# A sparse-attention layer on one core: query rows made by a product in the first steps, and another order around tile 0 in the last ones

## The chip, the cores and the metric

The kernel runs on 1 core of one Trainium2 chip. The metric is the device time in microseconds of one execution. The engines are TensorE (PE, with its weight loads on PEld), VectorE (DVE), ScalarE (ACT), GpSimd (POOL) and the engine that issues DMAs (SP). POOL also issues DMAs; its queue is called q0 here, SP's q1.

## What is computed

One layer of a graph transformer on 4096 nodes with 256 features, 8 heads of 32, fp32. The adjacency matrix is sparse: an edge (i, j) exists with a chance that falls with i and j, so the first rows have many neighbours and the last few.

```
mask = adj + eye(n)
q, k, v = h @ Wq.T + bq, h @ Wk.T + bk, h @ Wv.T + bv        # 8 heads of 32
scores = einsum(q, k) / sqrt(32), -1e9 where mask == 0
ctx = softmax(scores) @ v
h1 = layer_norm(h + ctx @ Wo.T + bo) * g1 + b1
h2 = layer_norm(h1 + relu(h1 @ W1.T + b1) @ W2.T + b2) * g2 + b2
```

## The kernel before

The 4096 rows are 32 tiles of 128. Up to about 66 us the key and value rows of all tiles are projected and stored in a table in HBM (`kv_table`), and the query rows of the first tiles in `q_table`. Then 19 **steps** follow (`STEPS`, numbered 0 to 18). Steps 0 to 3 treat tiles 4 to 7, one each; steps 4 to 15 two tiles each; steps 16, 17 and 18 the tiles 1, 2 and 3, with 3, 3 and 2 units. A unit is a stretch of columns of one tile. Tile 0, the densest, has 14 units and is no step of its own: it is worked off beside the others.

For each step:
- POOL loads 128 rows of the adjacency matrix as bytes (`load_adj`, a DMA that casts, two to three steps ahead), and VectorE **searches** them (`find_dve`, lines 533 and 537) for up to eight neighbours a row and unit. `columns_dve` and `spill_dve` make lists of them. The first neighbour of a row is treated as *aligned* with the row; the rest spill over and are packed as *edges*.
- TensorE and ScalarE make a selection matrix `rt` for packed slots (`starts_pe` L882, `distance_act`, `rt_dve`), then `lists_pe` (L889) and `cols_dve` give the column numbers of the edges, `rows_act` their row numbers, and `onehot_act` the transposed selection.
- POOL **gathers** with indirect DMAs: `gather_aligned` (L1084), `gather_edges` (L1096: key and value rows of the edges) and `gather_queries` (L1104: the query row of each edge, from `q_table`), one instruction a unit. SP loads the tile's own rows and queries (`load_own`).
- VectorE multiplies queries by keys and sums (`edge_scores_dve`, L687; `own_scores_dve`, L702), TensorE brings the edge scores to their rows (`ell_pe`, L901), VectorE takes the maximum and subtracts (`masked_dve`), ScalarE the exponential, VectorE the reciprocal (`norm_probs_dve`). TensorE hands maximum and reciprocal back to the edges (`tr_pe`, L909); VectorE weights the value rows (`own_sum_dve` with L783, `edge_weight_dve` with L792), and TensorE adds them up (`sum_pe`, L927 and L930).

Each engine runs its instructions in the written order; a wait stops all behind it. In steps 0 to 2 TensorE also has the query projections of the later tiles (`project_q`, four pairs of tiles a step, L1869 and L1872). From step 4 on it has the dense part of finished groups of four tiles, a **job**: attention output (L1153, with the residual through L1141), a transpose (L1163), the first feed-forward product (`post_pe_ff`, eight parts, L1173) and the second (`post_pe_out`, one a tile, L1186). They are cut into the gaps between a step's sparse matmuls (`dense(gap)`); two steps make one job. ScalarE takes the results (L1223), VectorE the statistics (L1243), POOL the root and the gain and bias of the second norm (`post_pool_gain` L1291, `post_pool_final` L1295).

**Tile 0** is scored in seven pieces of two units, in steps 8 to 14 (`score0_dve`, `masked0_dve`; their gathers in steps 6 to 12). In step 15 VectorE takes the maximum over its 1800 scores a row (`below0_dve`, L838), subtracts it (L840), ScalarE takes the exponential, and VectorE the sum (`norm0_dve`, L846). At the end of step 15 TensorE hands it to the 14 units (`tr0_pe`, L959), in step 16 and 17 VectorE weights the rows (`weight0_dve`, L868 and L871), and in step 17 TensorE adds them up (`sum0_pe`, L971, two halves back to back). In steps 16 to 18 the jobs 5 and 6 are finished by tables of their own (`late_ff`, `late_out`); S in the code is 16, W is 6. After step 18 two small jobs of two tiles follow, and `last_dve` ends the last.

## Time and profile before

| | us |
|---|---|
| three runs | 538.21, 535.16, 538.68 |
| median | 538.21 |
| the profiled execution: its time | 536.31 |
| its span, first to last instruction | 534.1 |
| PE busy | 474.5 (89%) |
| DVE busy | 389.7 (73%) |
| POOL busy | 270.3 (51%) |
| ACT busy | 216.0 (40%) |

The span lies 2.2 us under its execution's time. "Busy" is the sum of instruction times on an engine; a matmul at half clock counts longer. The granted TensorE clock over the span is 0.936 of full speed; the lows lie in steps 0 to 4 and 16 to 18. A row by stretch (rows 2) gives the stretch, its length, then the busy us of PE, PEld, DVE, ACT and POOL with the number of instructions each, the granted TensorE clock, the DMA share and GB/s. A row of a timeline gives start, duration, engine, line and operands. The waits in brackets name what ended the idle time of an engine just before an instruction.

### The profile page before, as it was taken

The numbers are of one execution on the slowest core, as the hardware profiler recorded it, in microseconds if no ns is written. First come the engines' busy times: TensorE is split into PE (matmuls) and PEld (weight loads), VectorE is DVE, ScalarE is ACT, GpSimd is POOL, SyncE is SP. The second block draws the span as 40 slices with busy tenths as digits, with TensorE's granted clock in tenths as the row PEclk, the third lists the DMA queues.
The fourth block names the chain that finished last, engine by engine and source line by source line (L and its number), as shares of the span: only waits on it lengthen the run. The fifth ranks groups of instructions, "written<-read, shape, count | busy, mean of one in ns | idle before, by whom it ended". The sixth has DMA issues, their size and how long they took to land.

```text
span 534.1 us, 7363 instructions
## 1 busy us (share of the span) xinstructions
PE 474.5 (89%) x2274; PEld 373.1 (70%) x2274; DVE 389.7 (73%) x1067; ACT 216.0 (40%) x533; POOL 270.3 (51%) x374
## 2 busy tenths in 40 slices
PE   5999978894389989999999999999999986999893
PEld 4888867783376677589578668758847864778682
DVE  0648825979788869799989979979969798713103
ACT  1243431443535334723624543373373436223530
POOL 7544454544334346777576657665455557300402
PEclk9999997986577989999999999999999888999997
DMA  7999869999979978999989898994673435100101
GB/s 181 282 285 311 233 205 221 288 255 233 281 157 214 173 168 140 236 223 198 228 144 221 201 171 205 138 242 149 114 160 97 129 91 152 56 1 1 40 0 43
DMA packets 42571, 91.66 MB, mean 172 GB/s; under 512 B 4888, under 2 KB 20632, under 8 KB 42400
## 3 DMA queue, kind: packets, MB, share of 16 engines
q0 software_dynamic: 16512, 55.60, 53.3%
q1 hardware_dynamic: 24224, 33.69, 18.1%
q10 hardware_dynamic: 1792, 1.85, 1.0%
q8 instruction: 20, 0.33, 0.3%
q14 instruction: 23, 0.19, 0.1%
HBM read 123.09 MB, written 16.80 MB: 262 GB/s over the span
## 4 chain that ended last, share of the span: by engine, by line
PE 62%; DVE 14%; issue 9%; ACT 6%; POOL 5%; DMA 4%; POOLq 0%; ACTq 0%; DVEq 0%
PE ps L1173 17%; PE ps L1186 14%; PE ps L1853 10%; PE ps L1153 6%; PE ps L927 2%; PE ps L1141 2%; DVE adj_bytes L533 2%; DVE adj_bytes L537 2%; DMA work<-q_table,row_of 2%; PE ps L971 2%; PE ps L930 1%; PE ps L1163 1%; POOL slots L1096 1%; DMA early<-in_wqkvT 1%; ACT early L1233 1%
## 5 line engine op out<-in xcount | busy, mean ns | idle before, releaser
L1186 PE MATMUL ps<-w,xT_all 128*128 128x256 f32 x512 | 118.4, 385 | 4.3 <-ACT xT_all L1223 2.6
L1173 PE MATMUL ps<-xT_all,w 128*128 128x512 f32 (+1 forms) x288 | 117.9, 554 | 2.6 <-ACT xT_all L1223 1.4
L1186 PEld LDWEIGHTS ps<-w,xT_all 128*128 128x128 f32 x512 | 95.8, 192 | 17.9 <-ACT xT_all L1223 3.8
L1096 POOL DMA_INDIRECT slots<-kv_table,col_of x54 | 53.4, 989 | 68.6 <-DVE col_of L613 53.9
L1173 PEld LDWEIGHTS ps<-xT_all,w 128*128 128x128 f32 x288 | 52.3, 192 | 47.2 <-issue 40.1
L1084 POOL DMA_INDIRECT slots<-kv_table,found x48 | 51.0, 1063 | 50.1 <-PE ps L930 26.1
L1223 ACT ACTIVATE xT_all<-ps,col_table 128x512 f32<-128x512 f32 (+1 forms) x72 | 45.8, 642 | 57.1 <-PE ps L1173 56.0
L1853 PE MATMUL ps<-early,xT_all 128*128 128x256 f32 x256 | 59.7, 394 | 6.1 <-DMA early<-in_wqkvT 6.1
L1853 PEld LDWEIGHTS ps<-early,xT_all 128*128 128x128 f32 x256 | 49.9, 198 | 14.0 <-DMA xT_all<-in_xT 4.7
L533 DVE MAX8 adj_bytes<-adj_bytes 128x8 f32<-128x1024 f32 (+5 forms) x40 | 38.2, 973 | 17.4 <-DMA adj_bytes<-in_adj 17.4
L1104 POOL DMA_INDIRECT work<-q_table,row_of x40 | 42.1, 1052 | 13.8 <-issue 13.8
L1243 DVE BATCH_NORM_STATS2 stats<-ps 128x6 f32<-128x256 f32 x62 | 22.2, 418 | 29.9 <-PE ps L1141 29.8
L1153 PE MATMUL ps<-wo,xT_all 128*128 128x256 f32 x128 | 39.3, 435 | 4.1 <-issue 4.1
L1282 POOL TENSOR_TENSOR rstd<-mv,eps_col 128x4 f32<-128x4 f32 (+1 forms) x17 | 5.8, 343 | 71.8 <-DVE mv L1249 71.5
L1039 ACT ACTIVATE xT_all<-ps,col_table 128x256 f32<-128x256 f32 (+1 forms) x38 | 14.4, 432 | 65.9 <-PE ps L930 65.9
L537 DVE FIND_INDEX8 adj_bytes<-adj_bytes 128x8 uint32<-128x1024 f32 (+5 forms) x40 | 38.9, 979 | 0.0
L927 PE MATMUL ps<-work,slots 128*128 128x128 f32 x160 | 29.0, 293 | 9.7 <-DVE slots L792 8.0
L1869 PE MATMUL ps<-early,xT_all 128*128 128x256 f32 x128 | 37.4, 419 | 0.0
L1608 POOL TENSOR_TENSOR slots<-slots,early 128x512 f32<-128x512 f32 x16 | 20.3, 1266 | 28.3 <-ACT slots L1700 28.3
L927 PEld LDWEIGHTS ps<-work,slots 128*128 128x128 f32 x160 | 24.6, 205 | 11.3 <-DVE slots L792 8.8
L1700 ACT COPY slots<-ps 128x1024 f32<-128x1024 f32 x16 | 16.2, 1012 | 39.3 <-PE ps L1853 39.3
L1153 PEld LDWEIGHTS ps<-wo,xT_all 128*128 128x128 f32 x128 | 25.1, 217 | 7.1 <-issue 4.6
(185 smaller groups left out, 856.4 us busy)
## 6 DMA issues: line engine op xcount, KB each, us to landing
adj_bytes<-in_adj POOLq DMA_DIRECT2D x31, 512.0 KB
kv_table<-slots POOLq DMA_DIRECT2D x7, 1024.0 KB, 13.0
xT_all<-in_xT SPq DMA_DIRECT2D x13, 512.0 KB, 30.8
slots<-kv_table SPq DMA_DIRECT2D x12, 512.0 KB
out_dram<-early SPq DMA_DIRECT2D x7, 512.0 KB
q_own<-q_table SPq DMA_DIRECT2D x12, 256.0 KB
slots<-in_adj SPq DMA_DIRECT2D x1, 2048.0 KB, 24.5
q_table<-slots SPq DMA_DIRECT2D x8, 256.0 KB
```

The costliest lines, as they stand in the source:

```text
L533: nc.vector.max(top_words[:, u, :], words[:, lo:hi]).then_inc(hunt, 1)
L537: last = nc.vector.max_index(word_at[:, u, :], top_words[:, u, :], words[:, lo:hi])
L927: nc.tensor.matmul(to, edge_slots(q)[:, c, feats], onehot[q.par][:, c, :], start=(u == 0), stop=False)
L1084: nc.gpsimd.indirect_dma_start(to, None, kv_dram, bass.IndirectOffsetOnAxis(ap=idx, axis=0)).then_inc(got_aligned[q.par], 16)
L1096: nc.gpsimd.indirect_dma_start(edge_slots(q)[:, u, :], None, kv_dram, bass.IndirectOffsetOnAxis(ap=col_of[q.par][:, u:u + 1], axis=0)).the ...
L1104: nc.gpsimd.indirect_dma_start(q_edge[q.par][:, u, :], None, q_dram[q.no // 2], bass.IndirectOffsetOnAxis(ap=row_of[q.par][:, u:u + 1], ax ...
L1153: nc.tensor.matmul(to, q["ctxT"][:, k, j * P:(j + 1) * P], wo[:, k, :], start=(k == 0), stop=False)
L1173: last = nc.tensor.matmul(ps[:, q["bank"] + f % 2, 0:q["g"] * P], w1[:, k, f * P:(f + 1) * P], q["h1T"][:, k, :], start=(k == 0), stop=(k ...
L1186: nc.tensor.matmul(to, q["ffT"][:, f, j * P:(j + 1) * P], w2[:, f, :], start=(f == 0), stop=False)
L1223: nc.scalar.activation(q["ffT"][:, f, :], ps[:, q["bank"] + f % 2, 0:q["g"] * P], ACT.Relu, bias=bias_1[:, f:f + 1]).then_inc(q["ff"], 1)
L1853: last = nc.tensor.matmul(ps[:, kv_bank(i, part), j * D:(j + 1) * D], xT_all[:, c, k, r * P:(r + 1) * P], wqkv[:, k, (1 + part) * D:(2 + p ...
L1869: nc.tensor.matmul(to, xT_all[:, c, k, r * P:(r + 1) * P], wqkv[:, k, 0:D], start=(k == 0), stop=False)
```

## The change

It has two halves.

**Steps 0 to 3** (`by_product`). The query rows of the edges are no longer gathered from HBM. TensorE multiplies the selection matrix `rt` by the tile's own queries (`queries_pe`), into the PSUM bank that holds nothing else then, and VectorE multiplies the keys by that. The product of step i+1 stands at the end of TensorE's step i. The searches of steps 2 and 3 are made before step 0, and steps 0 to 3 make one search each for steps 4 and 5 in place of none, one, two and two. In steps 1 to 3 VectorE makes the selection matrix and columns of the next step (`rt_dve`, `cols_dve`) earlier, before and after its own product, and TensorE `lists_pe` right behind `ell_pe`. Two constant rows of `kv_table` are counted on another semaphore.

**Tile 0 and steps 14 to 18.** The pieces lie one step earlier (gathers in steps 5 to 11, scores in 7 to 13). Each piece takes its own maximum; in step 14 a reduction over nine columns a head joins them, the subtraction becomes the bias of eight exponentials, one a head, that also give the sums. The 14 products of `tr0_pe` stand between the feed-forward parts of step 15, both weightings at the end of step 15, and the two halves of `sum0_pe` in steps 16 and 17, in a bank of their own. In steps 16 to 18 VectorE makes the next step's lists first, and statistics and search after its weighting; the first two feed-forward parts of job 6 move from step 16 to 17. POOL's gain and bias of a second norm stand together: in step 15 behind the gathers, in step 17 behind VectorE's weighting. The second norm of jobs 6 and 7 goes from ScalarE to VectorE (`post_dve_norm`), and `last_dve` has two instructions on the output in place of three.

The diff, cut to its core:

```diff
-GATHER0, SCORE0 = 6, 8
+GATHER0, SCORE0 = 5, 7
...
+        def by_product(q):
+
+            return q.b < FIRST_JOB
...
+            if by_product(q):
+                dve.wait_ge(queries_ps, q.b + 1)
+                nc.vector.tensor_tensor(qe, ps[:, ELL2, 0:q.U * D].rearrange("p (u d) -> p u d", d=D), keys, ALU.mult).then_inc(edge_product, 1)
+            else:
+                nc.vector.tensor_tensor(qe, qe, keys, ALU.mult).then_inc(edge_product, 1)
...
+        def own_product_dve(dve, q):
...
+            if by_product(q):
+                dve.wait_ge(own_queries, (q.b + 1) * 16)
...
+            dve.wait_ge(scoring0, 5 * i + 4)
+            nc.vector.tensor_reduce(tops0[:, :, i], slots0()[:, :, 1 + 2 * i * q.k:1 + (2 * i + 2) * q.k], AX_X, ALU.max).then_inc(scoring0, 1)
...
+            dve.wait_ge(softmax0, 2)
+            nc.vector.tensor_copy(tops0[:, :, PIECES0], slots0()[:, :, 0]).then_inc(softmax0, 1)
...
-            s = slots0()
...
-            nc.vector.tensor_reduce(tops, s, AX_X, ALU.max).then_inc(softmax0, 1)
-            dve.wait_ge(softmax0, 3)
-            nc.vector.tensor_tensor(s, s, tops.unsqueeze(2).to_broadcast([P, HEADS, TILE0.S]), ALU.subtract).then_inc(softmax0, 1)
+            nc.vector.tensor_reduce(tops, tops0, AX_X, ALU.max).then_inc(softmax0, 1)
+            dve.wait_ge(softmax0, 4)
+            nc.vector.tensor_scalar(below0, tops, -SCALE, None, ALU.mult).then_inc(softmax0, 1)
...
-            nc.vector.tensor_reduce(total_p0[:], s, AX_X, ALU.add).then_inc(softmax0, 1)
...
+        def queries_pe(pe, q):
+            pe.wait_ge(own_queries, (q.b + 1) * 16)
+            pe.wait_ge(rt_ready, q.b + 1)
+            wait(pe, edge_product, q.b)
+            for u in range(q.U):
+                last = nc.tensor.matmul(ps[:, ELL2, u * D:(u + 1) * D], rt[q.par][:, u, :], q_own[q.par][:, 0, :], start=True, stop=True)
+            last.then_inc(queries_ps, 1)
...
-        def tr0_pe(pe):
...
+            for u in us:
                 last = nc.tensor.matmul(tr0_out()[:, u, :], rt[TILE0.par][:, u, :], top_rec0[:], start=True, stop=True)
-            last.then_inc(psum0, 1)
+            if us[-1] == TILE0.U - 1:
+                last.then_inc(psum0, 1)
...
-            to = ps[:, ACC, k * 2 * P:(k * 2 + 1) * P]
+            to = ps[:, ELL2, k * P:(k + 1) * P]
...
         def probs0_act(act):
-            act.wait_ge(softmax0, 4)
-            nc.scalar.activation(scores0[:], scores0[:], ACT.Exp, scale=SCALE).then_inc(exp0, 1)
+            act.wait_ge(softmax0, 5)
+            for h in range(HEADS):
+                s = slots0()[:, h, :]
+                last = nc.scalar.activation(s, s, ACT.Exp, bias=below0[:, h:h + 1], scale=SCALE, accum_out=total_p0[:, h:h + 1])
+            last.then_inc(exp0, 1)
...
+        def load_own_queries(sp, q):
+            queries_ready(sp, q)
+            wait(sp, acc_ps, q.before)
+            if by_product(q):
+                wait(sp, queries_ps, q.b)
+            sp.dma_start(q_own[q.par][:, 0:q.T, :], q_tiles[q.no // 2][:, q.no % 2:q.no % 2 + q.T, :]).then_inc(own_queries if by_product(q) else own_loaded[q.par], 16)
...
+            if by_product(q):
+                load_own_queries(sp, q)
...
+        def post_dve_norm(dve, q, n):
+
+            dve.wait_ge(q["rstd2"], n + 1)
+            wait(dve, q["stored"], n * 16)
+            for j in range(q["g"]):
+                last = nc.vector.tensor_scalar(q["out"][:, j, :], tile_out(q, q["bank"] + 2, j), q["rstd"][1][:, j:j + 1], q["shift"][1][:, j:j + 1],
+                                               ALU.mult, ALU.add)
+            last.then_inc(q["norm2"], 1)
...
+            nc.vector.scalar_tensor_tensor(o, y, moments[:, 0:1], rows["g2"][:], ALU.subtract, ALU.mult).then_inc(q["mul2"], 1)
             dve.wait_ge(q["rstd2"], j + 1)
-            nc.vector.tensor_scalar(o, y, moments[:, 0:1], r, ALU.subtract, ALU.mult).then_inc(q["norm2"], 1)
-            dve.wait_ge(q["norm2"], j + 1)
-            nc.vector.tensor_tensor(o, o, rows["g2"][:], ALU.mult).then_inc(q["mul2"], 1)
             dve.wait_ge(q["mul2"], j + 1)
-            nc.vector.tensor_tensor(o, o, rows["be2"][:], ALU.add).then_inc(q["final"], 1)
+            nc.vector.scalar_tensor_tensor(o, o, r, rows["be2"][:], ALU.mult, ALU.add).then_inc(q["final"], 1)
 
...
         def late_ff(i, gap):
 
-            return {(S, 4): (W, (0, 1)), (S + 1, 1): (W, (2,)), (S + 1, 2): (W, (3, 4)), (S + 1, 3): (W, (5, 6)),
-                    (S + 1, 4): (W, (7,))}.get((i, gap), (0, ()))
+            return {(S + 1, 1): (W, (0, 1)), (S + 1, 2): (W, (2, 3)), (S + 1, 3): (W, (4, 5)),
+                    (S + 1, 4): (W, (6, 7))}.get((i, gap), (0, ()))
...
+                if place == 0 and n >= 0 and i < S:
+                    post_pool_rstd(pool, JOBS[n], n, 0)
+                if soon and not by_product(soon):
+                    gather_queries(pool, soon)
+                if i == S:
+                    post_pool_rstd(pool, JOBS[W], W, 0)
                 if apart(q):
                     pool.wait_ge(own_probs, i + 1)
                     pool.wait_ge(s_small, 16 * (SMALL_DMAS + ROW_DMAS))
                     post_pool_gain(pool, JOBS[n - 1], n - 1)
-                if soon:
-                    gather_edges(pool, soon)
-                if place == 0 and n >= 0:
-                    post_pool_rstd(pool, JOBS[n], n, 0)
...
-                if i >= 1 and apart(STEPS[i - 1]):
-                    post_pool_final(pool, JOBS[finished(STEPS[i - 1])], finished(STEPS[i - 1]))
                 if i == S + 1:
+                    post_pool_rstd(pool, JOBS[W - 1], W - 1, 1)
+                    pool.wait_ge(edge_weighted, 2 * i + 2)
                     post_pool_gain(pool, JOBS[W - 1], W - 1)
                     post_pool_final(pool, JOBS[W - 1], W - 1)
...
                 dense(3)
+                if i == WEIGHTS0:
+                    edge_exp0_act(act)
...
+                        for f in ff_gap(place, gap, i):
+                            post_pe_ff(pe, now, n, (f,))
+                            if i == WEIGHTS0 and 3 <= f <= 6:
+                                tr0_pe(pe, range(4 * (f - 3), min(4 * (f - 2), TILE0.U)))
...
+                if 0 < i < FIRST_JOB:
+                    lists_pe(pe, STEPS[i + 1])
...
-                if i > 0:
+                if i >= FIRST_JOB:
...
+                if i == S - 1:
+                    starts_pe(pe, STEPS[i + 2])
...
+                if by_product(STEPS[i + 1]):
+                    queries_pe(pe, STEPS[i + 1])
...
-                    post_pe_attn(pe, JOBS[W], W, ctx_ready, S, (0, 1))
-                dense(1)
+                    post_pe_attn(pe, JOBS[W], W, ctx_ready, S, (0,))
                 if soon:
                     lists_pe(pe, soon)
                 if i == S:
-                    post_pe_attn(pe, JOBS[W], W, ctx_ready, S, (2, 3))
+                    post_pe_attn(pe, JOBS[W], W, ctx_ready, S, (1, 2, 3))
+                dense(1)
+                if i == S + 1:
+                    dense(2)
                 tr_pe(pe, q)
-                if i == SUM0:
-                    for k in range(KC):
-                        sum0_pe(pe, k)
-                dense(2)
-                if i == S:
-                    post_pe_h1(pe, JOBS[W], W)
+                if i != S + 1:
+                    dense(2)
...
-                dense(3)
+                if i == S + 1:
+                    dense(3)
+                    sum0_pe(pe, 1)
...
+                if i == S:
+                    dense(3)
+                    post_pe_h1(pe, JOBS[W], W)
                     starts_pe(pe, STEPS[i + 2])
+                    sum0_pe(pe, 0)
...
             find_dve(dve, STEPS[2], 0)
+            columns_dve(dve, STEPS[2])
+            find_dve(dve, STEPS[3], 0)
+            columns_dve(dve, STEPS[3])
...
+                lists_first = 0 < i < FIRST_JOB or i >= S and soon
                 edge_scores_dve(dve, q)
+                if lists_first:
+                    rt_dve(dve, soon)
+                own_product_dve(dve, q)
+                if lists_first:
+                    cols_dve(dve, soon)
                 own_scores_dve(dve, q)
...
-                if i == WEIGHTS0 + 1:
-                    weight0_dve(dve, 1)
+                if i == SCORE0 + 4:
+                    own0_dve(dve)
                 if i == SOFTMAX0:
-                    own0_dve(dve)
                     below0_dve(dve)
+                if i >= S:
+                    own_weight_dve(dve, q)
+                    edge_below_dve(dve, q)
+                    if i == S + 1:
+                        post_dve_stats(dve, JOBS[W - 1], W - 1, 1)
+                    if i == S + 2:
+                        post_dve_stats(dve, JOBS[B1], B1, 0)
+                    own_sum_dve(dve, q)
+                    edge_weight_dve(dve, q)
+                    if i == S:
+                        post_dve_stats(dve, JOBS[W], W, 0)
+                        find_dve(dve, later, 0)
+                        columns_dve(dve, later)
+                        spill_dve(dve, later)
+                    continue
                 if place == 0 and n >= 0:
...
+                if i < FIRST_JOB:
+                    find_dve(dve, STEPS[FIRST_JOB + i // 2], i % 2)
+                else:
                     find_dve(dve, later, 0)
...
+                edge_below_dve(dve, q)
+                own_weight_dve(dve, q)
+                own_sum_dve(dve, q)
+                edge_weight_dve(dve, q)
                 if i == WEIGHTS0:
                     edge_below0_dve(dve)
-                edge_below_dve(dve, q)
-                own_sum_dve(dve, q)
-                edge_weight_dve(dve, q)
...
+                if i < FIRST_JOB:
+                    if i % 2:
+                        columns_dve(dve, STEPS[FIRST_JOB + i // 2])
+                else:
...
                     weight0_dve(dve, 0)
-                if later and later.T > 1 and i > 0:
-                    find_dve(dve, later, 1)
-                if later:
-                    columns_dve(dve, later)
-                    spill_dve(dve, later)
+                    weight0_dve(dve, 1)
...
+            post_dve_norm(dve, a, na)
```

Where the order moves. TensorE from the end of step 0 to the middle of step 1, before; L927 and L930 are `sum_pe`, L882 `starts_pe`, L1869 and L1872 half a pair of `project_q`, L901 `ell_pe`, L889 `lists_pe`:

```order
L927 MATMUL ps<-work,slots 128x128 x2
L930 MATMUL ps<-ident,slots 128x128
L882 MATMUL ps<-spill,minus_before 128x2
L1869 MATMUL ps<-early,xT_all 128x256 x2
L1872 MATMUL ps<-ident,scores0 128x128 x2
L1869 MATMUL ps<-early,xT_all 128x256 x2
L1872 MATMUL ps<-ident,scores0 128x128 x2
L901 MATMUL ps<-work 128x56 x2
L1869 MATMUL ps<-early,xT_all 128x256 x2
```

and now, the same stretch:

```order
L951 MATMUL ps<-work,slots 128x128 x2
L954 MATMUL ps<-ident,slots 128x128
L908 MATMUL ps<-spill,minus_before 128x2
L964 MATMUL ps<-q_own,work 128x256 x2
L1917 MATMUL ps<-early,xT_all 128x256 x2
L1920 MATMUL ps<-ident,scores0 128x128 x2
L1917 MATMUL ps<-early,xT_all 128x256 x2
L1920 MATMUL ps<-ident,scores0 128x128 x2
L927 MATMUL ps<-work 128x56 x2
L915 MATMUL ps<-idx_all,work 128x9 x2
```

The query product (L964) stands behind the sum and the starts of the step before, and the lists (L915) directly behind L927, which is `ell_pe` now.

TensorE in step 17, before; L1173 are feed-forward parts, L909 `tr_pe`, L971 and L972 the halves of `sum0_pe`:

```order
L1173 MATMUL ps<-xT_all,w1 128x512 x4
L901 MATMUL ps<-work 128x56 x3
L1173 MATMUL ps<-xT_all,w1 128x512 x2
L889 MATMUL ps<-idx_all,work 128x9 x2
L909 MATMUL ps<-top_rec,work 128x16 x3
L971 MATMUL ps<-work,slots 128x128 x14
L972 MATMUL ps<-ident,slots 128x128
L971 MATMUL ps<-work,slots 128x128 x14
L972 MATMUL ps<-ident,slots 128x128
L1173 MATMUL ps<-xT_all,w1 128x512 x8
```

and now:

```order
L1003 MATMUL ps<-work,slots 128x128 x14
L1004 MATMUL ps<-ident,slots 128x128
L927 MATMUL ps<-work 128x56 x3
L915 MATMUL ps<-idx_all,work 128x9 x2
L1217 MATMUL ps<-xT_all,w1 128x512 x8
L935 MATMUL ps<-top_rec,work 128x16 x3
L1217 MATMUL ps<-xT_all,w1 128x512 x4
L1003 MATMUL ps<-work,slots 128x128 x14
L1004 MATMUL ps<-ident,slots 128x128
```

Four feed-forward parts now stand between the lists and `tr_pe` (L935), where one stood before, and one half of `sum0_pe` (L1003) ahead of the step.

## Rows read from the trace of the kernel before

**Rows 1.** Page, part 4: the chain that ended last, by engine.

```profile
PE 62%; DVE 14%; issue 9%; ACT 6%; POOL 5%; DMA 4%; POOLq 0%; ACTq 0%; DVEq 0%
```

**Rows 2.** Busy time by stretch: steps 0 to 3, 8, 15, 16, 17.

```profile
79.00:94.60 15.60, 12.78 (x59) 10.82 (x60) 9.25 (x29) 2.73 (x8) 7.68 (x9) 0.78 1.00 223
94.60:109.90 15.30, 13.46 (x76) 11.35 (x76) 12.37 (x41) 7.18 (x24) 8.69 (x9) 0.92 1.06 294
109.90:125.40 15.50, 11.38 (x67) 9.58 (x65) 14.77 (x42) 5.11 (x14) 5.59 (x7) 0.94 0.94 231
125.40:143.50 18.10, 7.13 (x28) 6.16 (x28) 14.93 (x43) 7.23 (x24) 8.57 (x10) 0.50 1.02 249
...
233.90:256.40 22.50, 21.32 (x130) 18.40 (x129) 21.74 (x58) 9.74 (x26) 15.02 (x18) 1.00 0.96 208
...
387.70:413.50 25.80, 24.32 (x95) 15.21 (x94) 20.67 (x50) 13.82 (x31) 15.12 (x15) 1.00 0.59 133
413.50:440.20 26.70, 24.10 (x137) 21.19 (x137) 23.00 (x64) 10.44 (x29) 13.81 (x14) 0.87 0.36 109
440.20:460.50 20.30, 15.61 (x86) 12.48 (x85) 17.56 (x30) 8.20 (x22) 14.82 (x12) 0.83 0.40 117
```

**Rows 3.** Timeline of DVE: start, us, instruction [idle before <- releaser].

```profile
79.02 0.69 DVE L687 TENSOR_TENSOR work<-work,slots 128x512 f32<-128x512 f32 x1 [10.56 <-DMA work<-q_table,row_of]
83.61 0.96 DVE L702 TENSOR_TENSOR slots<-slots,q_own 128x768 f32<-128x768 f32 x1 [2.87 <-DMA slots<-kv_table,found]
...
143.52 0.69 DVE L687 TENSOR_TENSOR work<-work,slots 128x512 f32<-128x512 f32 x1 [2.36 <-DMA work<-q_table,row_of]
```

**Rows 4.** Timeline of PE, around step 0 and at the end of step 1.

```profile
66.05 1.03 PE L1869 MATMUL ps<-early,xT_all 128*128 128x256 f32 x4
...
80.80 1.10 PE L901 MATMUL ps<-work 128*128 128x56 f32 x4 [3.75 <-issue]
81.69 2.03 PE L1869 MATMUL ps<-early,xT_all 128*128 128x256 f32 x4
...
106.28 0.71 PE L927 MATMUL ps<-work,slots 128*128 128x128 f32 x4 [1.83 <-DVE slots L792]
```

**Rows 5.** Timeline of DVE in step 2: one search.

```profile
116.19 1.22 DVE L533 MAX8 adj_bytes<-adj_bytes 128x8 f32<-128x1024 f32 x1
...
117.52 1.22 DVE L537 FIND_INDEX8 adj_bytes<-adj_bytes 128x8 uint32<-128x1024 f32 x1
```

**Rows 6.** Timeline of POOL: an adjacency load, then a query gather of step 4.

```profile
127.30 0.61 POOL L1122 DMA_DIRECT2D adj_bytes<-in_adj  x1
...
135.22 1.04 POOL L1104 DMA_INDIRECT work<-q_table,row_of  x1 [0.30 <-issue]
```

**Rows 7.** Timeline of PE in steps 16 to 18.

```profile
413.80 3.28 PE L959 MATMUL ps<-top_rec,work 128*128 128x16 f32 x28
...
431.46 1.67 PE L1163 MATMUL ps<-ident,xT_all 128*128 128x128 f32 x8 [2.60 <-ACT xT_all L1233]
...
452.27 5.02 PE L971 MATMUL ps<-work,slots 128*128 128x128 f32 x28 [0.78 <-DVE slots L871]
```

**Rows 8.** Timeline of DVE in steps 15 to 17 and at the end.

```profile
400.17 2.03 DVE L838 TENSOR_REDUCE top_rec<-scores 128x8 f32<-128x1800 f32 x1
...
430.38 1.34 DVE L783 TENSOR_TENSOR slots<-slots 128x256 f32<-128x256 f32 x3
...
453.54 5.95 DVE L783 TENSOR_TENSOR slots<-slots 128x256 f32<-128x256 f32 x3
...
524.52 0.54 DVE L1262 TENSOR_SCALAR early<-ps,mv,rstd 128x256 f32<-128x256 f32 x1 [1.97 <-POOL rstd L1271]
```

**Rows 9.** Timeline of POOL in step 17.

```profile
454.35 2.37 POOL L1291 TENSOR_TENSOR early<-early,row_g 128x1024 f32<-128x1024 f32 x1
456.80 2.42 POOL L1295 TENSOR_TENSOR early<-early,row_be 128x1024 f32<-128x1024 f32 x1
```

**Rows 10.** Timeline of PE in the tail.

```profile
497.78 4.10 PE L1173 MATMUL ps<-xT_all,w 128*128 128x256 f32 x16 [1.03 <-ACT xT_all L1223]
```

138 lines of the change are left out of this document (68 added, 70 removed).

## The prediction, made before the changed kernel ran

> **What bounds the kernel now.** I read the chain of waits first: TensorE holds 62% of it, VectorE 14%, and 9% is issue [rows 1]. Then the busy time by stretch. A middle step (8) takes 22.5 us with TensorE busy for 21.32 at the full clock: there only less TensorE work would help. Two places look different. Steps 0 to 3 take 15.6, 15.3, 15.5 and 18.1 us, and TensorE is busy for 12.78, 13.46, 11.38 and 7.13 of them at clocks 0.78 to 0.94 and, in step 3, 0.50. Steps 15 to 17 take 25.8, 26.7 and 20.3 us, TensorE busy for 24.32, 24.10 and 15.61, at 1.00, 0.87 and 0.83 [rows 2]. These two are what the change touches.
>
> In step 0 VectorE waits 10.56 us for the last query gather and 2.87 more for the aligned gathers; step 4 again starts on a query gather [rows 3]. In steps 1 to 3 VectorE is busy for 12.37, 14.77 and 14.93 us, in step 2 nearly throughout [rows 2].
>
> **Start and step 0.** The four query gathers of steps 0 and 1 go. One occupies POOL for 1.04 us and 0.30 before it [rows 6], so the aligned gathers of step 0 are issued two gathers, 2.6 us, earlier; they release L702 at 83.61 [rows 3]. What replaces the first wait is short: two 128x256 products of TensorE cost what a half pair of projections costs, 1.03 us at the full clock and 2.03 at half [rows 4], behind the projections of 66 to 75 us. Step 0 also gains a search (1.22 + 1.22 us, [rows 5]), but of its 15.6 us VectorE is busy for only 9.25, so the search is hidden in what is left beside those waits; if the aligned gathers came with no delay at all, it would show as 2.4. The searches of steps 2 and 3 fill the 10.56 us before step 0: free. I let step 1 start 1.9 us earlier, 0.7 less than the gathers give.
>
> **Steps 1 to 3.** Step 1 trades one search for one, steps 2 and 3 make one in place of two: -2.5 us each, and some 0.8 us of list work leaves step 2 (estimate: a few small instructions beside a search). VectorE's work becomes 12.3, 11.5 and 12.4 us. The new order has a **round trip**: VectorE's last weighting, then on TensorE the sum (two blocks of 0.71 us and two transposes, about 1.3), the starts (0.3, estimate) and the product (1.03), 2.7 us with the signals about 2.9, while VectorE has 0.6 to 1.4 us of list work left. It adds 1.5 to 2.3 us a step at the full clock and about 4.5 at half. With one more microsecond of waits inside a step the periods are 14.7, 14.8 and, in the colder step 3, 16 to 17. Steps 1 and 2 gain 0.6 and 0.7: step 3 starts 3.2 us earlier. Step 4 keeps its query gathers. They stand in POOL's queue behind an adjacency load issued at 127.30 and release step 4 at 143.52 [rows 3, 6]: 16.2 us after that issue. The load now goes out about 4.2 us earlier, since it stands behind the aligned gathers, which wait for the sum of step 2 only. **Early: -4.5 us**; ends 0 (the round trip takes all) and -8 (VectorE's work alone sets the periods).
>
> **The middle.** Seven pieces each add a maximum over 256 scores, about 0.4 us of VectorE (estimate: a seventh of L838's 2.03 for 1800, [rows 8], and a start). In step 8 VectorE is busy for 21.74 of 22.5 us, and its partner step has more room [rows 2]; TensorE runs behind it, so I cost the pieces at nothing, and 3 us if VectorE is what paces. The piece that moves from step 14 to step 7 moves its matmuls with it: zero.
>
> **Steps 14 to 17.** VectorE loses three passes of 2.03 us over tile 0 in step 15 [rows 8] (the last, L846, and the subtraction are as long) and takes both weightings there, about 4.9 us. ScalarE's one exponential becomes eight with sums, a form that the trace does not show: at least 0.35 us each (3 in all), at most about 0.8 (6.4). It runs beside VectorE's search; I take 3.2 us, and up to 2 us late above that. In step 15 TensorE gets the 14 products (3.28 us, [rows 7]), where it idles for 1.5.
>
> What can be won in steps 15 to 17 I read from the stretches: idle 1.5 + 2.6 + 4.7 = 8.8 us, and time lost to the clock (1 - 0.87) x 26.7 + (1 - 0.83) x 20.3 = 3.5 + 3.5 us, together 15.8 [rows 2]. The idle pieces are the wait for the norm before the transpose (2.60), for the reciprocals of step 17 and for the second weighting (0.78), behind which `sum0` ran its first half in 5.02 us where the half clock held [rows 7]. In the new order the transpose stands behind two output tiles and a sum, the reciprocals behind four feed-forward parts, and the weighting two steps back. L783 in step 17 took 5.95 us where the same form took 1.34 in step 16 [rows 8], while POOL's gain and bias ran (2.37 + 2.42, [rows 9]); in the new order they wait until VectorE has weighted. **What is left** I put at 5.5 us: 0.8 for step 15 (next paragraph), 0.7 for `tr_pe` of step 16, which waits for a VectorE chain of about 9.5 us from the step's start, 0.7 for ScalarE's last results before the output tiles, and about 3 for stretches at half clock behind such gaps. So 15.8 - 5.5 = **-10.3 us**; ends 0 and -14.
>
> In step 15 gain and bias now stand together, 4.8 us, behind the gathers of step 16. By my count they start when VectorE is about to weight tile 0 and hold it for some 3 us; TensorE has one output tile, a sum and another tile to do, so 0.8 us shows. By the Trainium skill (SBUF — State Buffer, Who interferes with whom) a VectorE instruction with two inputs in SBUF and a GpSimd instruction that reads SBUF exclude one another for a whole instruction; the trace agrees, 5.95 against 1.34 us. Without that rule the same paragraph would give -11.1.
>
> **The tail.** ScalarE's norm of job 6 stands before the results that TensorE waits for, 1.03 us [rows 10]; it moves to VectorE, which is idle there: -1.0. At the end the first of the three output instructions (0.54 us after a wait of 1.97 for POOL, [rows 8]) goes beside the root, and two become one: about -1.2. **-2.2 us**, ends -1 and -3.
>
> **Sum.** 536.3 - 4.5 - 10.3 - 2.2 = 519.3 us for the profiled execution. That one lies 1.9 us under the median of 538.21, and the runs spread over 3.5; I predict **520 us** for the median. A change of less than 1%, 5.4 us, is about what cannot be told from none.
>
> **Rivals.**
> 1. *The round trip eats the early gain* (chance 0.15). For it: steps 3 and 4 had TensorE at half clock. Then early is 0 and the time 524.
> 2. *The lock and the clock halve the late gain* (0.17). If POOL's 4.8 us fall on the weighting of step 15 itself, TensorE waits for the sum and comes back at half clock: 4.8 + 2 us, the time 527. Against it: POOL has six gathers to issue first.
> 3. *It is absorbed* (0.06). The adjacency loads (DMA share 0.94 to 1.06 in steps 0 to 3, [rows 2]) or VectorE in the middle set the pace, and the late order brings half: 3 + 5 us at most, 531 to 537.
> 4. *Slower: TensorE stays at half clock in steps 0 to 3* (0.03). A half pair then takes 2.03 us and its transposes, 2.2 in place of 1.08 [rows 4]; four pairs 17.6 us, and with the six small groups at double length (about 8.7) a step takes 26.3, bound by TensorE, for three steps, and 17.5 for step 3: 96.4 us against 64.5, +32. With a start of -2.6 and the late gain, 554. It decides where the mean clock of steps 0 to 2 falls under about 0.7; against it stand 0.92 and 0.94 [rows 2], and the round trip adds a matmul group where there was none. The Trainium skill (TensorE: Matmul & The Clock Gate, Part 1) says that an idle TensorE falls to 1.2 GHz and a busy one comes back to 2.4; L901 at half clock behind 3.75 idle us agrees.
> 5. *More than forecast* (0.04): VectorE alone sets steps 1 to 3 and nothing is left over late, 513.
>
> **Numbers.** The forecast (both halves, 515 to 525) has 0.55. The range of 512 to 530 takes in rivals 1, 2 and 5 and leaves out 3 in part and 4. Faster by over 1% (under 532.8): 0.55 + 0.15 + 0.17 + 0.04 and a part of rival 3, 0.92; within 1%: 0.05; slower: 0.03.
>
> **What would show it.** In the profile after: the first product of edge scores near 76 us and the own product near 81; step 1 from about 92.7, steps 1 to 3 at 14 to 17 us each, step 4 from about 139. Wrong there: a start of step 4 at 143 or later, or adjacency loads named before the search. Late: steps 15 to 17 at about 25.5, 20 and 17 us, clock over 0.93, no wait over 1.5 us before the transpose or `tr_pe`, `sum0` halves of 3.3 us each. VectorE's weighting of tile 0 drawn out in step 15 by up to 3 us is in the forecast; TensorE waiting for the sum of step 15 is rival 2. Middle steps at over 23 us would make the pieces' maxima the step that failed.

## The result, and the profile after

Four runs of the changed kernel took 530.97, 531.37, 531.72 and 526.37 us, median **531.17**; the kernel before, beside it, 538.44 (four runs, 535.16 to 539.25). The ratio is 0.988, 95% interval 0.984 to 0.992: 1.2% faster, 7.3 us less by the medians. On another chip later (`after_again`, six runs) it came out the same, 528.79 against 535.86, ratio 0.9885 (0.985 to 0.992). The forecast was 520 with a range of 512 to 530: the sign was right, the size not, and the time lies outside the range. The profiled execution took 530.97 us, span 529.2, 4.9 us less than the span before. Ratios leave out executions that lie over 1.5% above the fastest of their kernel (two of the four of `e5_own_queries`, one each of `e6_step4`, `e8_lists_gain` and `e15_all_late`), which is why some ratios below do not match their medians.

The chain of waits by engine (page, part 4); [rows 1] answers to it.

```profile
PE 68%; DVE 14%; issue 7%; ACT 4%; POOL 3%; DMA 3%; ACTq 0%; SPq 0%; POOLq 0%; DVEq 0%
```

TensorE's share rose from 62 to 68% and issue fell from 9 to 7%. Where the 4.9 us came from shows in busy time by stretch: steps 0 to 3, 7, 8 and 14 to 17. Columns: window, length, busy us of TensorE, its weight loads, VectorE, ScalarE and POOL with counts, granted clock, DMA share, GB/s; [rows 2].

```profile
77.60:96.20 18.60, 14.20 (x65) 11.67 (x64) 10.78 (x27) 4.43 (x13) 6.58 (x8) 0.77 1.00 187
96.20:111.50 15.30, 13.13 (x76) 11.29 (x76) 12.22 (x37) 5.11 (x15) 3.37 (x5) 0.94 0.98 244
111.50:127.40 15.90, 13.64 (x78) 11.26 (x76) 11.62 (x34) 7.16 (x24) 5.39 (x7) 0.93 0.98 223
127.40:142.30 14.90, 5.47 (x23) 5.19 (x24) 12.59 (x40) 1.89 (x7) 5.33 (x6) 0.50 1.04 300
...
212.29:235.69 23.40, 22.97 (x94) 15.27 (x93) 20.90 (x44) 11.26 (x27) 17.67 (x17) 1.00 0.99 209
235.69:258.67 22.98, 21.79 (x131) 18.63 (x130) 22.19 (x58) 10.13 (x26) 15.41 (x18) 1.00 0.91 201
...
370.87:391.45 20.58, 18.95 (x101) 16.10 (x100) 17.07 (x61) 13.16 (x41) 8.62 (x11) 0.92 0.68 153
391.45:420.21 28.76, 27.14 (x125) 18.43 (x123) 22.98 (x48) 16.58 (x44) 20.60 (x19) 1.00 0.64 156
420.21:442.02 21.81, 19.45 (x88) 17.00 (x89) 16.80 (x52) 4.73 (x13) 8.48 (x12) 0.77 0.35 102
442.02:460.02 18.00, 18.00 (x93) 12.13 (x92) 12.96 (x37) 8.63 (x21) 8.09 (x10) 1.00 0.35 103
```

Counted from first product to first product, step 0 got 3.1 us longer (18.6), steps 1 and 2 hardly changed (15.6 each), step 3 got 3.2 shorter (14.9) and step 4 2.3 longer (25.2), step 14 got 1.5 longer (20.6) and step 15 2.9 (28.8), and steps 16 and 17 are 4.8 and 2.3 shorter. By the start of step 5 nothing is won (167.48 against 166.39), by step 14 2.3 us are lost, by step 18 0.5 won. The remaining 4.4 lie behind that point: 2.7 because TensorE reaches its first output tile there 8.3 us after VectorE's start of step 18 in place of 11.1, and 1.7 in the tail. DMA share is 0.98 to 1.04 in steps 0 to 3.

VectorE in steps 0 to 4: start, us, instruction [idle before <- releaser]; it answers to [rows 3].

```profile
77.58 0.69 DVE L703 TENSOR_TENSOR work<-ps,slots 128x512 f32<-128x512 f32 x1 [4.65 <-DMA slots<-kv_table,col_of]
81.87 0.96 DVE L722 TENSOR_TENSOR slots<-slots,q_own 128x768 f32<-128x768 f32 x1 [2.57 <-DMA q_own<-q_table]
...
90.72 0.69 DVE L817 TENSOR_TENSOR slots<-slots,p_edge 128x512 f32<-128x512 f32 x1
...
96.21 0.69 DVE L703 TENSOR_TENSOR work<-ps,slots 128x512 f32<-128x512 f32 x1 [4.37 <-PE ps L964]
...
100.09 0.16 DVE L605 TENSOR_SCALAR row_at<-ps 128x2 f32<-128x2 f32 x1 [0.90 <-PE ps L915]
...
111.84 0.69 DVE L703 TENSOR_TENSOR work<-ps,slots 128x512 f32<-128x512 f32 x1 [1.49 <-PE ps L964]
...
127.41 0.69 DVE L703 TENSOR_TENSOR work<-ps,slots 128x512 f32<-128x512 f32 x1 [3.00 <-PE ps L964]
...
142.30 0.69 DVE L705 TENSOR_TENSOR work<-work,slots 128x512 f32<-128x512 f32 x1 [0.64 <-DMA work<-q_table,row_of]
...
149.91 0.29 DVE L596 TENSOR_SCALAR work<-work,spill 128x128 f32<-128x128 f32 x1 [3.49 <-ACT idx_all L1023]
```

TensorE between the last weighting of step 0 and step 1; [rows 4] has the same blocks at full clock.

```profile
91.47 1.22 PE L951 MATMUL ps<-work,slots 128*128 128x128 f32 x4 [1.66 <-DVE slots L817]
...
94.05 2.05 PE L964 MATMUL ps<-q_own,work 128*128 128x256 f32 x4
```

The weighting ends at 91.41, TensorE comes out of 1.66 us of idle at half clock (the sum 1.22 in place of 0.71, the product 2.05 in place of 1.03), and step 1 can start at 96.21: a round trip of 4.8 us. In step 1 VectorE waits 0.90 us for the lists (L605); step 4 starts behind its query gather again and then waits 3.49 us for ScalarE. The row at 81.87 names the own queries, but TensorE had read them at 74.99 already; `after_again` names the aligned gathers there, which L722 waits for too.

POOL in step 3: the adjacency load, the first edge gather and the last query gather of step 4. They answer to [rows 6].

```profile
128.31 0.61 POOL L1166 DMA_DIRECT2D adj_bytes<-in_adj  x1
...
132.02 0.97 POOL L1131 DMA_INDIRECT slots<-kv_table,col_of  x1 [3.10 <-DVE col_of L616]
...
135.92 0.95 POOL L1139 DMA_INDIRECT work<-q_table,row_of  x1 [0.30 <-issue]
```

The load goes out 1.0 us later than before (127.30), the last query gather 0.7 later (135.22).

VectorE and POOL at the end of step 15, and TensorE behind it; they answer to [rows 7 to 9].

```profile
410.72 3.05 DVE L585 SCALAR_TENSOR_TENSOR idx_all<-found,row_ids 128x24 f32<-128x24 uint32 x1
...
413.87 2.55 DVE L894 TENSOR_TENSOR slots<-slots,scores 128x256 f32<-128x256 f32 x1
416.34 3.95 DVE L897 TENSOR_TENSOR slots<-slots,p_edge 128x1792 f32<-128x1792 f32 x2
```

```profile
411.35 2.36 POOL L1342 TENSOR_TENSOR early<-early,row_g 128x1024 f32<-128x1024 f32 x1
413.79 2.35 POOL L1346 TENSOR_TENSOR early<-early,row_be 128x1024 f32<-128x1024 f32 x1
```

```profile
422.57 1.53 PE L927 MATMUL ps<-work 128*128 128x56 f32 x6 [3.20 <-DVE work L712]
423.89 2.03 PE L1197 MATMUL ps<-wo,xT_all 128*128 128x256 f32 x4
...
443.77 3.37 PE L1003 MATMUL ps<-work,slots 128*128 128x128 f32 x28
...
459.17 3.29 PE L1003 MATMUL ps<-work,slots 128*128 128x128 f32 x28
```

POOL's gain and bias run from 411.35 to 416.14. L585 (L582 before, 0.23 us at 413.38) takes 3.05, ending with the gain (its record begins 0.6 us ahead of it; POOL's spans are rough), and the first weighting of tile 0 2.55. VectorE reaches step 16 at 420.21; TensorE, through with everything at 419.4, waits 3.20 us for it and then runs at half clock to about 432.

VectorE at the end, where [rows 8] had a wait of 1.97; the kernel before had three instructions per output tile there.

```profile
518.34 0.48 DVE L1314 SCALAR_TENSOR_TENSOR early<-ps,mv,row_g 128x256 f32<-128x256 f32 x1
520.36 0.48 DVE L1317 SCALAR_TENSOR_TENSOR early<-early,rstd,row_be 128x256 f32<-128x256 f32 x1 [1.55 <-POOL rstd L1322]
```

TensorE in the tail, which answers to [rows 10]: 28 matmuls in a row where a wait of 1.03 us stood before 16.

```profile
491.16 6.59 PE L1217 MATMUL ps<-xT_all,w 128*128 128x256 f32 x28
```

### The profile page after: what moved, and what is told of

It is laid out like the page before. It is cut to its first block, busy times and chain, and to the rows that moved or that the text cites. A ratio compares the mean times of both kernels' runs of the same rounds, so it can differ in the third digit from the quotient of the medians.

```text
span 529.2 us, 7430 instructions
## 1 busy us (share of the span) xinstructions
PE 478.4 (90%) x2290; PEld 377.9 (71%) x2290; DVE 390.5 (74%) x1078; ACT 214.9 (41%) x538; POOL 260.7 (49%) x366
## 4 chain that ended last, share of the span: by engine, by line
PE 68%; DVE 14%; issue 7%; ACT 4%; POOL 3%; DMA 3%; ACTq 0%; SPq 0%; POOLq 0%; DVEq 0%
PE ps L1217 19%; PE ps L1230 15%; PE ps L1901 10%; PE ps L1197 5%; PE ps L951 3%; PE ps L1185 2%; PE ps L954 2%; DVE adj_bytes L540 2%; DVE adj_bytes L536 2%; PE ps L927 2%; PE ps L915 1%; PE ps L1207 1%; DMA early<-in_wqkvT 1%; PE ps L1003 1%; PE ps L974 1%
## 5 line engine op out<-in xcount | busy, mean ns | idle before, releaser
L1217 PE MATMUL ps<-xT_all,w 128*128 128x512 f32 (+1 forms) x288 | 117.3, 551 | 0.7 <-ACT xT_all L1250 0.6
L1230 PEld LDWEIGHTS ps<-w,xT_all 128*128 128x128 f32 x512 | 94.8, 190 | 18.6 <-ACT xT_all L1267 5.4
L1217 PEld LDWEIGHTS ps<-xT_all,w 128*128 128x128 f32 x288 | 52.1, 191 | 43.4 <-issue 38.9
L1119 POOL DMA_INDIRECT slots<-kv_table,found x48 | 49.4, 1028 | 62.7 <-PE ps L954 43.2
L1901 PE MATMUL ps<-early,xT_all 128*128 128x256 f32 x256 | 59.9, 396 | 6.0 <-DMA early<-in_wqkvT 6.0
L1197 PE MATMUL ps<-wo,xT_all 128*128 128x256 f32 x128 | 41.7, 457 | 4.6 <-issue 4.6
L1139 POOL DMA_INDIRECT work<-q_table,row_of x32 | 36.0, 1126 | 12.5 <-issue 10.3
L1287 DVE BATCH_NORM_STATS2 stats<-ps 128x6 f32<-128x256 f32 x62 | 22.1, 417 | 24.2 <-PE ps L1185 24.2
L1917 PE MATMUL ps<-early,xT_all 128*128 128x256 f32 x128 | 35.0, 398 | 0.0
L1197 PEld LDWEIGHTS ps<-wo,xT_all 128*128 128x128 f32 x128 | 26.7, 231 | 7.9 <-issue 5.1
```

The source lines that it names most:

```text
L1119: nc.gpsimd.indirect_dma_start(to, None, kv_dram, bass.IndirectOffsetOnAxis(ap=idx, axis=0)).then_inc(got_aligned[q.par], 16)
L1139: nc.gpsimd.indirect_dma_start(q_edge[q.par][:, u, :], None, q_dram[q.no // 2], bass.IndirectOffsetOnAxis(ap=row_of[q.par][:, u:u + 1], ax ...
L1197: nc.tensor.matmul(to, q["ctxT"][:, k, j * P:(j + 1) * P], wo[:, k, :], start=(k == 0), stop=False)
L1217: last = nc.tensor.matmul(ps[:, q["bank"] + f % 2, 0:q["g"] * P], w1[:, k, f * P:(f + 1) * P], q["h1T"][:, k, :], start=(k == 0), stop=(k ...
L1230: nc.tensor.matmul(to, q["ffT"][:, f, j * P:(j + 1) * P], w2[:, f, :], start=(f == 0), stop=False)
L1901: last = nc.tensor.matmul(ps[:, kv_bank(i, part), j * D:(j + 1) * D], xT_all[:, c, k, r * P:(r + 1) * P], wqkv[:, k, (1 + part) * D:(2 + p ...
```

## The experiments

All but `after_again` change the kernel after. Step starts are VectorE's first product of edge scores in the profiled execution, as in the text above; "late" is from the start of step 14 to that of step 18. `after` has 0.984 to 0.992 and `after_again` 0.985 to 0.992, and an interval that reaches into these is not clear of the changed kernel: that goes for every single edit below. Clear of it are `e8_lists_gain`, `e10_adj_later`, `e11_products` and, by a hair, `e13_weights_late`.

```
kernel            median  before   ratio (95%)            step 4   step 5   step 14   late
before                                                    143.52   166.39   368.60   91.90
after             531.17  538.44   0.988 (0.984, 0.992)   142.30   167.48   370.87   89.15
after_again       528.79  535.86   0.989 (0.985, 0.992)   143.56   166.20   368.44   89.31
e1_product_first  530.37  536.46   0.990 (0.984, 0.996)   146.06   167.95   370.33   86.01
e2_lists_behind   526.95  536.46   0.981 (0.975, 0.988)   143.18   164.80   367.39   89.13
e3_gain_moved     526.07  536.46   0.980 (0.974, 0.987)   144.37   166.59   369.32   85.74
e4_late_only      528.06  536.46   0.983 (0.977, 0.989)   145.42   167.02   369.08   89.21
e5_own_queries    528.42  536.89   0.978 (0.971, 0.985)   148.40   170.00   372.57   89.10
e6_step4          528.14  536.89   0.982 (0.974, 0.990)   143.79   168.15   371.23   89.11
e7_fill14         527.98  536.89   0.987 (0.981, 0.994)   141.83   164.50   367.15   86.33
e8_lists_gain     521.52  536.89   0.971 (0.961, 0.981)   141.63   164.15   364.17   84.06
e9_weights        528.32  535.47   0.983 (0.978, 0.988)   147.15   170.61   373.99   85.61
e10_adj_later     522.22  535.47   0.972 (0.968, 0.977)   138.93   162.48   362.54   84.06
e11_products      522.46  535.47   0.973 (0.969, 0.978)   139.46   161.93   365.04   85.75
e12_late_gain     525.39  535.47   0.979 (0.973, 0.985)   143.57   165.71   368.74   85.74
e13_weights_late  523.73  535.86   0.979 (0.975, 0.983)   141.12   165.18   368.01   85.74
e14_all           525.36  535.86   0.981 (0.977, 0.985)   144.42   166.96   369.68   85.72
e15_all_late      526.65  535.86   0.982 (0.978, 0.987)   141.09   162.79   372.72   85.74
```

### The late half: gain and bias out of step 15

`e3_gain_moved`, in POOL's program:

```diff
-                if apart(q):
+                if apart(q) and i < S - 1:
...
+                if i == S:
+                    done = finished(STEPS[S - 1])
+                    pool.wait_ge(own_scores, 2 * i + 1)
+                    post_pool_gain(pool, JOBS[done], done)
+                    post_pool_final(pool, JOBS[done], done)
```

> The changed kernel, with POOL's gain and bias of step 15 moved into step 16, behind VectorE's own product and ahead of the edge gathers. Theory A (the lock halved the late gain): VectorE's L585 (3.05 us) and the first L894 (2.55) in step 15 shrink to about 0.25 and 0.45, step 16 starts 4.9 us earlier, TensorE's 3.20 us wait for it is gone and with it most of the half clock that followed for 10 us: 3.2 + 4 us, time 523 to 526. In step 16 the two land on a stretch in which VectorE waits for the lists. Rival B (TensorE would have lost the clock and the time anyway, or the gathers of step 17 come 4.8 us later and hold it up): 529 to 532.

Measured: 526.07, 4.4 us less than the changed kernel by the ratios. VectorE at the same place, and the stretches of steps 15 to 17:

```profile
409.17 0.23 DVE L585 SCALAR_TENSOR_TENSOR idx_all<-found,row_ids 128x24 f32<-128x24 uint32 x1
...
409.50 0.42 DVE L894 TENSOR_TENSOR slots<-slots,scores 128x256 f32<-128x256 f32 x1
...
422.14 2.17 DVE L746 TENSOR_TENSOR scores<-scores,mask 128x24 f32<-128x24 f32 x1
```

```profile
389.91:413.70 23.79, 23.01 (x105) 15.01 (x104) 18.02 (x48) 12.54 (x31) 12.60 (x14) 1.00 0.64 143
413.70:436.02 22.32, 19.40 (x106) 16.88 (x104) 18.86 (x51) 7.96 (x25) 15.88 (x16) 0.92 0.46 135
436.02:455.06 19.04, 19.04 (x97) 13.04 (x97) 12.97 (x37) 9.40 (x23) 8.11 (x10) 1.00 0.35 113
```

L585 and the weighting are back at 0.23 and 0.42 us, step 15 takes 23.79 us in place of 28.76, and TensorE does not wait at the start of step 16. Theory A holds for the lock (4.97 us). 1.6 us come back in steps 16 and 17: L746 now takes the blow (2.17 us where it took 0.20), and TensorE has 2.92 us of idle in the middle of step 16, with clock 0.92. Steps 14 to 17 are 3.4 us shorter than in the changed kernel. The time itself is less clear than the rows: 0.974 to 0.987 against 0.984 to 0.992.

`e7_fill14` puts an output tile where the piece had stood:

```diff
+            if g == STEPS[LATE - 2].group:
+                return {0: (2,), 3: (3,)}.get(gap, ())
             return {2: (2,), 3: (3,)}.get(gap, ())
```

> The changed kernel, with one output tile of step 14 moved on TensorE to the start of that step, where the piece of tile 0 stood before the change moved it to step 7. Theory: without the piece TensorE idles 1.10 + 0.33 us there and then runs 7 us at half clock, so that step 14 takes 20.6 us in place of 19.1; with the gap filled it takes 18.7 to 19.2: time 529.5. Rival: step 14 is longer for VectorE's and ScalarE's work on the softmax of tile 0 (eight exponentials, 3.7 us): it keeps 20.6 us, and so does the time.

Step 14 kept its length (20.83 us) though TensorE ran at the full clock at its start: it then waited 2.05 us for ScalarE, whose norm stands behind the eight exponentials. The rival holds for this order, and the ratio, 0.987, is the changed kernel's. (The half clock in step 14 of the changed kernel lasted some 3.4 us, by a granted clock of 0.83 from 369 to 379, not the 7 us of my expectation.) The theory is not dead for the other one: in five kernels whose step 14 is that of the changed kernel (`e1_product_first`, `e8_lists_gain`, `e9_weights`, `e10_adj_later`, `e14_all`) the same 1.10 + 0.33 us of idle left the clock at 1.00, and step 14 took 18.9 us; in the others with the same step 14 it took 20.6. TensorE at that place in the changed kernel and in `e8_lists_gain`:

```profile
372.63 0.65 PE L927 MATMUL ps<-work 128*128 128x56 f32 x4 [1.10 <-DVE work L712]
...
375.05 1.92 PE L1197 MATMUL ps<-wo,xT_all 128*128 128x256 f32 x4
```

```profile
365.94 0.65 PE L927 MATMUL ps<-work 128*128 128x56 f32 x4 [1.10 <-DVE work L712]
...
368.07 1.03 PE L1197 MATMUL ps<-wo,xT_all 128*128 128x256 f32 x4
```

The same output block took 1.92 us in the one and 1.03 in the other. So 1.7 us hang on whether the clock falls there. Step 6 is a second such place: in `e8_lists_gain` and `e10_adj_later` it ran at a granted clock of 1.00 and took 22.9 and 23.1 us, in all others, the kernel before too, it took 24.2 (at 0.93 in `before`, `after` and nine more). No edit here touches step 6. The table shows it as the distance from step 5 to step 14: 200.0 and 200.1 us in these two, 202.1 to 203.4 in the others (`e15_all_late` apart).

### The early half

`e2_lists_behind`:

```diff
-                if 0 < i < FIRST_JOB:
-                    lists_pe(pe, STEPS[i + 1])
...
-                if i >= FIRST_JOB:
+                if i > 0:
                     lists_pe(pe, STEPS[i + 1])
...
-                lists_first = 0 < i < FIRST_JOB or i >= S and soon
+                lists_first = i >= S and soon
```

> The changed kernel, with the list work of steps 1 to 3 (the compare before the own product and the columns before the own scores) put back behind the own scores, on VectorE and on TensorE, as it was before. Theory: VectorE's 0.7 to 0.9 us wait for the lists and the 0.4 us wait for the exponential, which the columns used to hide, go: from the start of a step to its last weighting 11.7 in place of 12.9 us, so 3.6 us over the three steps, time 527 to 528. Rival: the wait only moves into the round trip behind the last weighting, or the edge gathers issued later land too late; time 530 to 532.

526.95, 3.7 us less by the ratios. Both waits are gone, as VectorE in step 2 shows (the columns fill the exponential's time and no idle stands before either row):

```profile
116.40 0.16 DVE L605 TENSOR_SCALAR row_at<-ps 128x2 f32<-128x2 f32 x1
...
116.96 0.28 DVE L767 TENSOR_REDUCE total_p<-scores 128x8 f32<-128x136 f32 x1
```

Step 2 takes 14.25 us in place of 15.57. But step 4 starts no earlier (143.18 against 142.30), behind its query gather again: with the lists behind the scores the last query gather goes out 9.9 us after the start of step 3, and 8.5 in the changed kernel, so the order gives back there what it won. By the start of step 5 the profile has 2.7 us less, and only 1.4 less than `after_again`. That the waits go is shown; that this is what shortens the time is not.

`e8_lists_gain` is both edits together.

> e2_lists_behind and e3_gain_moved together (the lists of steps 1 to 3 behind the own scores; POOL's gain and bias of step 15 in step 16). They touch different stretches, so by both theories their gains add up: 2.7 us by the start of step 5 and 5.0 in step 15, time 522 to 523. Rival: part of one gain was chance between runs of the same kernel (their spread is 3 us), 525 to 526.

521.52 us, ratio 0.971: **2.9% faster than before, and by the two ratios (0.971, 0.988) 1.7% faster than the change as it was made**. The gains add up: 3.7 + 4.4 us apart, 9.2 together by the ratios. Part of it is luck with the clock: the profile has 1.7 us from it in step 14 and 1.3 in step 6. `e13_weights_late` below, the same kernel but for two weight loads, has neither and came out at 0.979 (0.975 to 0.983).

`e4_late_only` takes the early half out (queries gathered, searches and lists in the old order: by_product returns False and what follows from it):

> The change without its early half: queries of steps 0 to 3 gathered, searches and lists in the old order; the late half and the tail as changed. Theory: the early half brought nothing (step 5 started at 167.5 after and 166.4 before), so the time is 530 to 531, the same as with both halves. Rival: the early half moved something that the start of step 5 does not show (adjacency loads, clock), and without it the time is 534 or more.

528.06, ratio 0.983, 2.6 us under the changed kernel where I expected the same; step 5 starts at 167.02, like there. The early half as made brought nothing; whether it cost something stays open, since the intervals overlap (0.977 to 0.989 against 0.984 to 0.992).

`e12_late_gain` is `e4_late_only` with the edit of `e3_gain_moved`.

> e4_late_only with e3_gain_moved: the change without its early half, and POOL's gain and bias of step 15 in step 16. Theory: the late half alone, with the lock taken away, gives all that the change gives and what the lock cost it: 528.1 less 5.0, time 523; the early half, mended (e8_lists_gain, 521.5), is then worth 1.5. Rival: without the early half step 5 starts 2 us or more later than there and the two differ by 3 or more: 525.

525.39: the rival's time, 3.9 us above `e8_lists_gain` by the medians and 4.2 by the ratios. By the start of step 5 the two are only 1.6 us apart (165.71 against 164.15), which is the theory's figure; behind it the profiles differ by 1.7 for the clock in step 14 and by 3.0 between step 5 and step 14, where no edit lies. So I put the mended early half at 1.6 to 4.2 us; the intervals of the two ratios overlap (0.973 to 0.985, 0.961 to 0.981), and the lower end is the better founded.

`e6_step4`:

```diff
                 if i == LISTS0:
+                    distance_act(act, STEPS[i + 2])
                     distance0_act(act)
...
-                if i == LISTS0 + 1:
-                    rt0_dve(dve)
...
                 norm_probs_dve(dve, q)
+                if i == LISTS0 + 1:
+                    rt0_dve(dve)
```

> The changed kernel, with another order at the edge of steps 3 and 4: ScalarE makes the distances of step 5 before the 14 of tile 0 (4.19 us), and VectorE makes tile 0's 14 row compares (2.83 us) behind the norm of step 4 in place of ahead of it. Theory: in the changed kernel step 4 took 25.2 us in place of 22.9, because VectorE waited 3.49 us for ScalarE, whose chain starts at the sum of step 3, which came 3.1 us later than before; with the new order the wait goes and step 4 takes 22 us: time 528. Rival: TensorE, at half clock in step 4, sets its length, and the 14 compares now hold up the matmuls behind the norm: no change, 530 to 532.

The wait for ScalarE went, and step 4 still took 24.36 us: VectorE now waited 2.56 us for TensorE's lists at half clock, and TensorE 2.47 us for the compares. By the profile the rival holds, by the median, 528.14, the theory's figure. Neither is firm: `after_again`, without this edit, has no wait for ScalarE in step 4 and takes 22.64 us there, so the 3.49 us may be the chance of one execution.

### Waits or transfers: what holds steps 0 to 3

`e1_product_first`:

```diff
+                if by_product(STEPS[i + 1]):
+                    queries_pe(pe, STEPS[i + 1])
                 sum_pe(pe, q)
...
                 if i < S - 1:
                     starts_pe(pe, STEPS[i + 2])
-                if by_product(STEPS[i + 1]):
-                    queries_pe(pe, STEPS[i + 1])
```

> The changed kernel, with the product that makes the next step's edge queries put in front of the sum on TensorE in steps 0 to 2, where TensorE idles 1.7 to 2.2 us, in place of behind the sum and the starts. Theory A (the round trip through the sum ate the early gain): steps 1, 2 and 3 start as soon as VectorE's list work is done, 4.3, 1.4 and 3.0 us less after the step before, together up to 8.7 us by the start of step 3; some comes back in step 4, which stands on ScalarE's chain behind the sum of step 3. Time 523 to 526. Rival B (the gathers and adjacency loads set the pace): VectorE then waits for the own rows or the edge gathers instead, and the time stays at 530 or above.

Step 1 started at 91.41, 4.8 us earlier, as theory A has it. Then TensorE:

```profile
109.79 2.07 PE L964 MATMUL ps<-q_own,work 128*128 128x256 f32 x4 [7.06 <-DMA q_own<-q_table]
```

The own queries of step 2, asked for at 96.67, landed at 109.79, and step 1 took 20.56 us. All of it was given back: 530.37. Neither theory had this wait; it is of rival B's kind.

`e5_own_queries` is `e1_product_first` with the own queries asked for earlier:

```diff
-            wait(sp, acc_ps, q.before)
             if by_product(q):
+                wait(sp, own_scores, 2 * q.before - 1)
                 wait(sp, queries_ps, q.b)
+            else:
+                wait(sp, acc_ps, q.before)
...
-            if by_product(q):
+            if q.b < 2:
                 load_own_queries(sp, q)
...
                         store_q(p)
+                    if gap == 2 and by_product(STEPS[min(i + 2, NB - 1)]):
+                        load_own_queries(sp, STEPS[i + 2])
```

> As e1_product_first (the product ahead of the sum in steps 0 to 2), and SyncE issues the own queries of steps 2 and 3 earlier: after the third query store of steps 0 and 1, near 89 us, in place of behind the fourth and behind the sum (96.7 us there, landed at 109.8, for which TensorE idled 7.06 us). Theory: the rows of own queries were the wait that took the place of the round trip; with them earlier step 1 keeps its 13.7 us, step 2 starts near 106, and step 4 near 140: time 525 to 527. Rival (the 16 DMA engines, at a share of about 1.0 from 80 us on, are the bound of steps 0 to 3): the rows land 11 to 13 us after their issue wherever they are issued, or the edge gathers do, step 4 starts at 143 or later and the time stays at 529 or above.

SyncE could issue the load at 98.64 only, because the store of the same rows (issued at 79.9) had to land first; the load landed at 110.50, 11.9 us after its issue. For the landing and for step 4 (148.40) the rival holds. The time does not decide: the profile is that of the longest of four executions, 523.21 to 532.72, and the ratio, 0.978, is the theory's. `e11_products` adds the earlier store to it, and both edits of `e8_lists_gain`:

```diff
             store_q(0)
             load_own(sp, STEPS[0])
+            store_q(1)
...
-            for i in range(1, Q_BEFORE):
+            for i in range(2, Q_BEFORE):
                 store_q(i)
```

> e8_lists_gain, with the product of the next step's queries ahead of the sum, as in e5_own_queries, and the query store of the second pair, which holds the queries of steps 2 and 3, issued before the wait for the first edge gathers. In e5_own_queries the own queries of step 2 could be asked for only at 98.6 us, once that store had landed, and came at 110.5. Theory: store and load both pass before 100 us, step 2 starts near 105 and not at 110 to 112, and the start of step 4 is set by its query gathers: 139 to 141, time 519 to 520. Rival (the DMA engines' total work sets the pace): the rows land late again and step 4 starts at 141 to 144, time 521 to 524.

Steps 1, 2 and 3 start at 93.17, 107.29 and 120.75, 13.5 to 14.1 us apart: VectorE is almost never idle there (1.53 and 0.78 us for the lists, 0.59 for an edge gather). Then VectorE, at step 4, and POOL's issue of what it waits for:

```profile
139.46 0.69 DVE L705 TENSOR_TENSOR work<-work,slots 128x512 f32<-128x512 f32 x1 [5.80 <-DMA work<-q_table,row_of]
```

```profile
130.31 1.05 POOL L1139 DMA_INDIRECT work<-q_table,row_of  x1 [0.30 <-issue]
```

VectorE was ready for step 4 at 133.7 and waited 5.80 us for the query gather; it starts 2.2 us before `e8_lists_gain` does, and 5.8 later than its own work allows. The places are the theory's except step 2, 107.29 for 105; the time, 522.46, is that of `e8_lists_gain` and in the rival's range, though in the profiles `e8_lists_gain` had the shorter step 14 (18.9 us against 20.6). Four more kernels vary the transfers, on top of `e8_lists_gain`.

`e10_adj_later`, each adjacency load one place later:

```diff
-            load_adj(pool, STEPS[4].h + 1)
             gather_edges(pool, STEPS[1])
             gather_aligned(pool, STEPS[1])
+            load_adj(pool, STEPS[4].h + 1)
...
```

> e8_lists_gain, with each adjacency load of steps 0 to 3 issued one place later in POOL's queue, behind the gathers instead of ahead of them; each was landed 10 us or more before its search. Theory (the transfers set the pace): the gathers and the rows of own queries land sooner since no 512-KB load stands ahead of them; step 1 starts 1 to 2 us earlier and step 4 near 139 to 140, time 519 to 520.5. Rival: the same bytes have to pass by step 4 anyway and only their order changes, or a search now waits for its load: step 4 at 141 or later, time 521 to 523.

`e9_weights`, wo, w1 and w2 before the first gathers:

```diff
+            sp.wait_ge(s_kv, PAIRS)
+            sp.dma_start(wo[:], ...)
+            sp.dma_start(w1[:], ...)
             store_q(0)
             load_own(sp, STEPS[0])
+            sp.dma_start(w2[:], ...)
```

> e8_lists_gain, with the loads of the three weight matrices (0.25 + 1 + 1 MB) moved by SyncE from steps 1 to 3 (issued at 108, 123 and 127 us) to 68 and 74 us, where the DMA engines' share is 0.2 to 0.5. Theory: the DMA engines are the bound of steps 0 to 3 (share about 1.0 from 80 to 142 us in every kernel so far, and step 4 starts at 141.6 to 148.4 whatever the order of the work), so what is taken from them there, 2.25 MB or about 6 us of all 16 engines, comes off the start of step 4, as far as VectorE allows: step 4 near 137 to 138 in place of 141.6, time 517.5 to 519. Rival: the clock and the engines' own chain set the pace, the share is only queueing: step 4 stays at 141 to 143, the first gathers may come later, time 521 to 524.

`e13_weights_late`, w1 and w2 in step 4 (`if i == 4:` in place of 2 and 3):

> e8_lists_gain, with the loads of w1 and w2 (1 MB each, issued at 123 and 127 us) moved behind the own rows of step 5, at about 141 us; w1 is first read near 163. Theory (the transfers hold step 4): the query gathers of step 4 share the engines with 2 MB less and land 2 to 3 us earlier, step 4 starts near 138.5 to 140: time 519 to 520. Rival: the gathers stand behind the adjacency load in their own queue and land when they did, 141 to 142, or w1 comes late and TensorE waits for it in step 4: time 521.5 to 525.

`e14_all` is `e8_lists_gain`, `e10_adj_later` and `e11_products` together:

> e8_lists_gain with e10_adj_later and e11_products together: lists behind the own scores, products ahead of the sums, adjacency loads behind the gathers, gain and bias in step 16. Theory: steps 1 to 3 start at 91, 104.5 and 118, as VectorE's work alone allows (13.4 us each), and step 4 is held by its query gathers, near 137 to 138: time 518 to 519.5. Rival: step 4 does not start before 139 to 141, and the time is that of the others, 521 to 522.

`e15_all_late` is `e14_all` with `e13_weights_late`:

> e14_all with w1 and w2 loaded late as in e13_weights_late. Theory (the transfers hold step 4): step 4 starts 2 to 4 us earlier than in e14_all, near 134 to 136, time 515 to 517. Rival (ScalarE's chain behind the sum of step 3, or the wait for w1, takes it back by step 5): step 5 starts when it did in e14_all, 518 to 520.

VectorE at the waits that decided in `e9_weights` (step 0) and `e14_all` (steps 2 and 4), and TensorE at the start of step 5 of `e15_all_late` (L1219 is L1217 of the changed kernel; in front of these matmuls the kernel has TensorE wait for w2):

```profile
86.32 0.69 DVE L703 TENSOR_TENSOR work<-ps,slots 128x512 f32<-128x512 f32 x1 [13.19 <-DMA slots<-kv_table,col_of]
```

```profile
111.41 0.69 DVE L703 TENSOR_TENSOR work<-ps,slots 128x512 f32<-128x512 f32 x1 [5.38 <-DMA slots<-kv_table,col_of]
...
144.42 0.69 DVE L705 TENSOR_TENSOR work<-work,slots 128x512 f32<-128x512 f32 x1 [5.64 <-DMA work<-q_table,row_of]
```

```profile
168.27 3.78 PE L1219 MATMUL ps<-xT_all,w 128*128 128x512 f32 x4 [3.92 <-DMA w<-in_w2T]
```

In `e10_adj_later` step 4 starts 2.7 us earlier in the profile (theory), but that is its fastest execution, 517.54, and the median, 522.22, is that of `e8_lists_gain` (rival). In `e9_weights` the 2.25 MB delayed the first edge gathers by 7.6 us (86.32 against 78.68) and only 2.1 came back by step 4: neither theory, the same load at a worse place. In `e13_weights_late` step 4 starts at 141.12, no earlier than 141.63: the rival, and so is the time, 523.73. In `e14_all` the waits are 5.38 us for edge gathers and 5.64 for query gathers; its time, 525.36, lies above both forecasts and above each of the three kernels that it joins. In `e15_all_late` step 4 starts 3.3 us earlier than in `e14_all` and step 5 4.2 earlier: the theory, where the rival had step 5 unchanged. Then TensorE waits 3.92 us for w2, issued at 140.20 and landed 28.0 us later, and step 5 takes 27.1 us in place of 20.4. w1 had landed: TensorE multiplies by it at 160.48. And w2 is first read at 183.55; the wait stands that far ahead of its use. So the time, 526.65, above both forecasts, is that of a wait at a needless place, not an answer to the question.

The idle of VectorE changes its place and releaser in every one, while the start of step 4 stays between 138.9 and 148.4, 143.5 before. POOL's rows split that start into two parts, the issue of the last query gather and the time from there to the start of the step:

```
kernel            step 3   last gather issued   step 4   issue to start
before            125.38   135.22 (+9.8)        143.52    8.3
after             127.41   135.92 (+8.5)        142.30    6.4
after_again       126.93   134.63 (+7.7)        143.56    8.9
e2_lists_behind   125.59   135.44 (+9.9)        143.18    7.7
e5_own_queries    128.52   137.61 (+9.1)        148.40   10.8
e8_lists_gain     125.13   134.96 (+9.8)        141.63    6.7
e10_adj_later     123.76   133.34 (+9.6)        138.93    5.6
e11_products      120.75   130.31 (+9.6)        139.46    9.2
e13_weights_late  126.16   136.00 (+9.8)        141.12    5.1
e14_all           125.86   135.43 (+9.6)        144.42    9.0
e15_all_late      122.94   132.78 (+9.8)        141.09    8.3
```

The gather goes out 7.7 to 9.9 us behind the start of step 3, since its indices come out of step 3's list work, and takes 5.1 to 10.8 us under a DMA share of about 1.0. So the start of step 4 is the engines' chain up to the issue plus a loaded transfer; that the transfers alone hold this stretch is not shown. How much is theirs these runs do not settle either: 2 MB less in flight made the second part 1.6 us shorter in one pair and 0.7 in the other, and two profiles of the changed kernel differ by 2.5.

> The changed kernel unchanged, beside the three others. If the gains of the mended kernels are real and not differences between chips, it comes out at 529 to 532, 8 us or more above them; if the first measurement was high by chance, at 526 to 528.

528.79, ratio 0.9885, the same as the first time, though below the range that I gave. The kernels measured beside it are 2.1 to 5.1 us lower, not 8; of them `e13_weights_late` (0.979) is clear of it. `e8_lists_gain` itself was not run again. So the gain of the mended kernels is not a difference between chips, and its size is not settled to better than some us. Its step 5 starts at 166.20 where the first profile had 167.48; kernels with the same early code gave 164.5 to 167.5 (`e7_fill14`, `e3_gain_moved`), so 3 us there are chance in a single profile.

## Why the prediction was wrong

By the terms of the sum, against the profiled execution: early -4.5 forecast, +1.1 measured (-0.2 in `after_again`); middle 0, +1.2 (0.0); steps 14 to 17 -10.3, -5.5 (from the start of step 14 to the first output tile behind step 17, 102.96 us before and 97.47 after); tail -2.2, -1.7. The measured terms make -4.9, the difference of the spans.

**The early term failed, at three steps of it, 5.6 us together.** The first is the start of step 1, 96.21 where I had 92.7: 1.6 us of it is the start of step 0 (77.58 for 76, released by an edge gather, which the prediction had put at nothing), 1.9 the round trip. I took 2.9 us for that, the full-clock price, in a step whose clock [rows 2] had at 0.78; it was 4.8, and my own half-clock figures would have been nearer. This is rival 1, to which I gave 0.15.

The second is "with one more microsecond of waits inside a step the periods are 14.7, 14.8". Both took 15.6. Step 1 was 12.22 us of VectorE's work (forecast 12.3), 0.90 of waiting for the lists, 0.41 for the exponential (together 1.31 for the forecast's 1), 1.49 for the product and 0.6 between instructions, which the sum had left out. In step 2 the wait for the product was 3.00 us, since it ran at half clock (2.04 us), for 2.3 in the sum. `e2_lists_behind` shows that the waits inside go with the order, and in `e8_lists_gain` steps 1 to 3 take 14.71, 14.99 and 16.50 us, the forecast's 14.7, 14.8 and 16 to 17.

The third is the path to step 4. "The load now goes out about 4.2 us earlier" did not happen: the aligned gathers do wait for the sum of step 2, but step 3 began 2.0 us later than before and not 3.2 earlier, and the load left at 128.31 for 127.30. That step 4 still started 1.2 us earlier (142.30, forecast 139.3) is luck in part: the last gather left 0.7 us later and took 6.4 us, and 8.9 in `after_again`, for 8.3 before. Step 4 itself was taken to keep its 22.9 us and took 25.2, with 3.49 of waiting for ScalarE; in `after_again` it took 22.6. So the early term was missed by 5.6 us in one profile and 4.3 in the other, and 2.3 of the first is step 4.

**Under it lies, in part, rival 3's first half.** The round trip and the lists could be mended, and what came out was a wait for a transfer each time (`e1_product_first`, `e5_own_queries`, `e11_products`, `e14_all`). The text had the DMA share of 0.94 to 1.06 before it, gave that case 0.06, and named 531 to 537 for it; the measured 531.17 alone would not tell it from rivals 1 and 2. But the wait is for a gather that is also issued late, so it is not the adjacency loads alone. By what the mended kernels show, the early half is worth 1.6 to 4.2 us, for 4.5 in the forecast and 8 at its far end.

**The late term failed at two steps, 4.8 us together: the lock in step 15, and the piece moved out of step 14.** For the lock, "so 0.8 us shows" was the sentence. The place was right and the hold was underrated: 2.8 us on L585, an instruction that I had not counted among those that the rule names, and 2.1 on the weighting, 4.95 for "some 3". What was wrong is who waits: I let TensorE have "one output tile, a sum and another tile to do", 4 + 1.3 + 4 us, and it had; but behind them came step 16's first product, which needs VectorE, not the sum of step 15. It waited 3.20 us and paid with half clock. This is rival 2 with another waiter: 4.8 + 2 us, where taking the lock out gave 3.4 in the profile and 4.4 by the ratios. Rivals 1 and 2 together would have given 520 + 4 + 7 = 531; I had weighed them one at a time. That this is the measured time is luck in its terms: the early half came out 1.1 us worse than rival 1's nothing, the middle 1.2 worse, and the late half 2 us better than rival 2's. The Trainium skill (SBUF — State Buffer, Who interferes with whom) has VectorE instructions with two inputs in SBUF and GpSimd instructions that read SBUF exclude one another; by that rule L585 is held as the weighting is, and the trace agrees, 3.05 against 0.23 us.

Without the lock the same stretch takes 94.06 us in `e3_gain_moved` and `e13_weights_late`, -8.9 for a forecast of -10.3, and 92.38 in `e8_lists_gain` and `e10_adj_later`, -10.6, where the clock in step 14 stayed up. That difference is the second step: moving the piece from step 14 to 7 was costed at zero, but its product had stood in TensorE's gap at the start of step 14 (1.11 us at 369.12 before). With the gap open the clock fell behind it in some executions and not in others, 1.7 us. That the open gap is the cause is argued from `e7_fill14`, which closes it and keeps the clock, in one profile.

Two slips in the sums changed little: what was left in steps 15 to 17 adds up to 0.8 + 0.7 + 0.7 + 3 = 5.2 us and not 5.5, and 519.3 for the profiled execution with 1.9 for the median is 521.2 and not 520.

**Right, or nearly:** the middle, with 0 to 1.2 us for seven maxima (step 7, which got the moved piece, 23.4 us for 22.7 before, over the 23 that I had named as a sign; step 8, 23.0 for 22.5); `sum0` halves of 3.37 and 3.29 us; steps 16 and 17 at 21.8 and 18.0 for 20 and 17. **The tail**, -1.7 for -2.2: the wait of 1.03 us is gone, and from the first output tile behind step 17 to the transposes in front of the last hidden layer it takes 29.25 us (468.34 to 497.59) for 30.17 before; the end is 0.8 us shorter and not 1.2, because the second of the two instructions still waits 1.55 us for the root.

## What to carry to other kernels

When a change removes a wait, look for the transfer that the next stage starts on, for what issues it and for the share of the DMA engines, before costing what is left on the engines: here VectorE could be made ready for step 4 7.5 us sooner (133.7 in `e11_products`, 141.2 before), but the gather was issued only 4.9 sooner (130.31, 135.22 before) and took 0.9 longer, so step 4 starts 4.1 sooner (139.46, 143.52 before). Two rivals that sit in different stretches add up; their joint case belongs in the range. A wait for a load stands best right ahead of the load's first reader (w2 in `e15_all_late`). Work on POOL that locks VectorE goes where VectorE waits anyway, and even there it can hit a small instruction (L746 in `e3_gain_moved`); the engine to ask about is the one that needs VectorE's *next* instruction, not the one being held.

## What was not expected of the hardware

The clock did not follow from the idle alone. `e7_fill14` has the same wait at the start of step 16 as the changed kernel, 3.22 against 3.20 us:

```profile
419.62 0.88 PE L927 MATMUL ps<-work 128*128 128x56 f32 x6 [3.22 <-DVE work L712]
420.33 1.09 PE L1197 MATMUL ps<-wo,xT_all 128*128 128x256 f32 x4
```

L927 took 0.88 us there and 1.53 in the changed kernel; the granted clock over the 10 us from its start was 1.00 against 0.50. At the start of step 14, 1.43 us of idle left the clock at 1.00 in five profiles and was followed by the half clock in the others of the same order. `after` has executions with mean clock 0.938 at about 531 us and one with 0.950 at 526.4.

A load of 128 KB of own queries, issued at 72.45 us, had been read by TensorE at 74.99, so it took 2.5 us at most. The same load took 13.1 (96.67 to 109.79) and 11.9 us (98.64 to 110.50) in step 1, where the DMA engines' share is about 1.0; TensorE's wait for it was 7.06 and 6.83 us.
